# A Mamba-2 layer on one core: front end on 256 tokens, convolution without a halo, y channel-major to the output projection, exponent factors placed by DMA

## What is computed

```python
xn = _layernorm(x)
out = x + attn(xn) + tanh(xn @ W1.T @ W2.T @ W3 + bias)      # the three-matrix branch

# attn:
z, xBC, dt = split(xn @ W_in, [512, 512 + 768])              # 8 values of dt, one per head
dt = softplus(dt + dt_bias)
xBC = silu(causal_conv(xBC, conv_w, 4 taps) + conv_b)
x, B, C = split(xBC, [512, 512 + 128])                       # x: 8 heads of 64
a = -exp(A_log)
y = ssd(x * dt, dt * a, B, C) + x * D                        # decaying state of 128 x 64 per head
y = y * silu(z)
y = y * rsqrt(mean(y * y) + EPS) * rms_w
h = xn + y @ W_out
return _layernorm(h) * ln_g + ln_b
```

## Time and profile before

| | |
|---|---|
| median of 3 runs | 756.85 us (755.51 to 758.68) |
| span of the profiled execution | 754.5 us |
| PE busy | 732.5 us, 5412 products |
| PE weight loads busy | 626.0 us |
| DVE busy | 699.9 us, 1568 instructions |
| ACT busy | 671.5 us, 1715 instructions |
| POOL busy | 644.3 us, 1226 instructions |
| data moved | 20.13 MB, 27 GB/s |

### The profile page before, as it was taken

One profiled execution on the slowest core, in us unless ns is written; L12 is line 12 of the kernel. 1 busy time (PEld: TensorE's weight loads), 2 busy tenths in 40 slices (PEclk: granted clock), 3 DMA queues, 4 the chain that ended last, 5 costly groups with the idle time before them and its releaser, 6 DMA issues. The chain is left out here.

```text
span 754.5 us, 19295 instructions
## 1 busy us (share of the span) xinstructions
PE 732.5 (97%) x5412; PEld 626.0 (83%) x5412; DVE 699.9 (93%) x1568; ACT 671.5 (89%) x1715; POOL 644.3 (85%) x1226
## 2 busy tenths in 40 slices
PE   5899999999999999999999999999999999999994
PEld 5778888888888888888888888888888888888873
DVE  3779999999999999999999999999999999999996
ACT  4798899999999999999999999999999999999993
POOL 6666989889888989888988988888988888988865
PEclk8899999999999999999999999999999999999999
DMA  6000010000000000000000000000000000000001
GB/s 203 17 1 15 14 45 4 28 30 29 28 28 13 15 28 28 28 28 28 0 28 28 28 28 28 0 28 28 28 28 28 11 17 28 28 28 14 14 1 42
DMA packets 21417, 20.13 MB, mean 27 GB/s; under 512 B 2832, under 2 KB 20880, under 8 KB 21392
## 3 DMA queue, kind: packets, MB, share of 16 engines
q1 hardware_dynamic: 20176, 19.82, 8.1%
q10 hardware_dynamic: 1216, 0.02, 0.1%
HBM read 11.45 MB, written 8.39 MB: 26 GB/s over the span
## 5 line engine op out<-in xcount | busy, mean ns | idle before, releaser
L849 DVE SCALAR_TENSOR_TENSOR u<-ring,cw,u 128x256 f32<-128x256 f32 x561 | 252.5, 478 | 3.3 <-ACT u L1425 0.6
L1753 PE MATMUL ring<-xhl,wh 128*128 128x262 f32 x748 | 153.0, 296 | 0.5 <-ACT vabs L1417 0.4
L1753 PE MATMUL ring<-wh,xhl 128*128 128x512 f32 (+1 forms) x512 | 147.6, 348 | 0.5 <-ACT gate L1445 0.4
L1753 PEld LDWEIGHTS ring<-xhl,wh 128*128 128x128 f32 x748 | 122.3, 191 | 12.6 <-DVE u L849 7.5
L1425 ACT ACTIVATE u<-ring,cb,cw 128x256 f32<-128x256 f32 x187 | 107.5, 576 | 26.1 <-PE ring L1753 23.8
L1485 ACT ACTIVATE xdt<-xt_bank,dts 128x64 f32<-128x64 f32 x512 | 111.2, 336 | 0.0
L1753 PE MATMUL ring<-xhl,wl 128*128 128x262 f32 x374 | 106.7, 285 | 0.0
L1753 PEld LDWEIGHTS ring<-wh,xhl 128*128 128x128 f32 x512 | 90.6, 189 | 10.9 <-issue 1.2
L869 DVE SCALAR_TENSOR_TENSOR lay<-e_bank,btg 128x512 f32<-128x512 f32 x125 | 85.9, 687 | 12.5 <-ACT e_bank L1468 10.3
L1753 PE MATMUL ring<-wl,xhl 128*128 128x264 f32 (+1 forms) x256 | 87.2, 341 | 0.0
L1468 ACT ACTIVATE e_bank<-e_bank 128x512 f32<-128x512 f32 x125 | 75.5, 604 | 2.4 <-PE e_bank L1877 1.1
(11 more groups left out here) (203 smaller groups left out, 2111.7 us busy)
## 6 DMA issues: line engine op xcount, KB each, us to landing
xin<-in_x_dram SPq DMA_DIRECT2D x32, 256.0 KB, 2.9
out_dram<-obuf SPq DMA_DIRECT2D x31, 256.0 KB, 3.0
lay<-in_w_in_dram SPq DMA_DIRECT2D x1, 776.0 KB, 5.1
lay<-in_w_in_dram SPq DMA_DIRECT2D x1, 512.0 KB, 9.9
wo<-in_w_out_dram SPq DMA_DIRECT2D x1, 512.0 KB, 5.7
lay<-in_f2t_dram SPq DMA_DIRECT2D x1, 256.0 KB, 6.7
lay<-in_f_dram SPq DMA_DIRECT2D x1, 256.0 KB, 8.6
lay<-in_f1t_dram SPq DMA_DIRECT2D x1, 256.0 KB, 8.9
```

The costliest lines, as they stand in the source:

```text
L849: v.scalar_tensor_tensor(out=u[:, ct], in0=conv_bank(k, ct)[:, :, t:t + P], scalar=cw[:, ct, t:t + 1], in1=u[:, ct], op0=ALU.mult, op1=ALU ...
L1753: last = mul(out, a, c, start=first and i == 0, stop=i == n - 1)
```

## The change

- A step now is 256 tokens (`C = 2` chunks of 128) for the front end: 16 steps, two buffers, a loop body for two steps. Norm scale, `transpose_x`, convolution, z, softplus and `sums` work on 256 tokens at once; the back end still goes chunk by chunk.
- No halo: `conv_project` makes 512 columns (2 sequences x 256). `conv_in` writes to `xs[..., 0:T]` and `tap` adds the bank's 512 columns into `xs` at an offset, so that the last three columns spill over its end; `save_spill` (POOL) keeps them and `join_spill` (DVE) adds them to the next step's first three columns. `u` is gone.
- The gate is made channel-major (`z_project`: four groups of 128 channels). y stays channel-major: `y_off` is four products of 128 channels each; `scale_off` multiplies with `grow`, the growth factor laid out for each channel and token; POOL's `join_skip` adds `x * D` to it; `add_diag` adds that to y; `apply_gate` works in PSUM; `y_skip`, `y_tokens`, `transpose_y` are gone. There is one `yd_bank`, two `e_bank`.
- Squares: `y_split` (ACT) writes `yts` and the squares, `fold` (DVE) adds four channel tiles in two additions, `square_sum` (PE) sums over the partitions, `mean_square` (DVE) adds EPS.
- `sums` (ACT) writes rows and their Exp (`growth`). SP places the factors: `spread_factors`, 16 transfers of 2 KB from `rows` into `left` and `right`, for each chunk, in place of `spread_rows`; `put_growth` writes `growth` to DRAM, and `spread_growth` reads it back, repeated for 64 partitions, two transfers of 128 KB for each chunk and sequence.
- Output is stored from `res`; `obuf` is gone.

The core of the diff (the orders of all engines are written anew; only the pieces that the text speaks of are shown):

```diff
-PH = HALO + P
+C = 2
+T = C * P
-BUF = 3
+BUF = 2
...
-            def y_tokens(k, q):
-                pe.wait_ge(t2_done[q], k + 1)
-                for ki in range(KI):
-                    last = tr(yd_bank[q][:, ki * P:(ki + 1) * P], yct[:, q, ki * P:(ki + 1) * P], ident[:, :])
-            def transpose_y(k, q):
...
-                v.scalar_tensor_tensor(out=u[:, ct], in0=conv_bank(k, ct)[:, :, t:t + P], scalar=cw[:, ct, t:t + 1],
-                                       in1=u[:, ct], op0=ALU.mult, op1=ALU.add).then_inc(tap_done[ct], 1)
+                to = xs[:, b, ct, :, HALO - t:HALO - t + T]
+                v.scalar_tensor_tensor(out=to, in0=conv_bank(j, ct), scalar=cw[:, ct, t:t + 1], in1=to,
+                                       op0=ALU.mult, op1=ALU.add).then_inc(tap_done[ct], 1)
...
+            def scale_off(j, b, c, q):
+                k = C * j + c
+                dve.wait_ge(yoff_in_psum[q], k)
+                dve.wait_ge(grow_loaded[q], 32 * k)
+                dve.wait_ge(y_done[q], k)
+                v.tensor_tensor(t1[:, q], xt_bank[:, :], grow[:, q].rearrange("p k t -> p (k t)"), ALU.mult).then_inc(t1_done[q], 1)
+            def fold(j, b, c, q):
+                v.tensor_tensor(sq[:, q, 0:2], sq[:, q, 0:2], sq[:, q, 2:4], ALU.add).then_inc(folded_done[q], 1)
+                dve.wait_ge(folded_done[q], 2 * k + 1)
+                v.tensor_tensor(folded[:, q], sq[:, q, 0], sq[:, q, 1], ALU.add).then_inc(folded_done[q], 1)
...
+                for ct in range(KI):
+                    block_of = slice(ct * P, (ct + 1) * P)
+                    last = mul(xt_bank[:, block_of], state[:, q, block_of], xs[:, b, KI + 1, q, tokens(c)], start=True, stop=True)
...
+                mul(ss_bank[:, q], folded[:, q], ones[:, 0:2], start=True, stop=True).then_inc(ss_in_psum, 1)
...
+            def exponents(j, b, c, q, half):
+                pe.wait_ge(factors_in[c], 256 * (j + 1))
...
+            def spread_factors(j, b, c):
+                k = C * j + c
+                sp.wait_ge(rows_done, j + 1)
...
+                for i in range(FOUR):
+                    for low in range(2):
+                        at, n = c * Q * H, 2 * FOUR * i + FOUR * low
+                        sp.dma_start(right[n:n + FOUR, c, i].bitcast(F32), rows[at + i:at + Q * H:FOUR, b, low].bitcast(F32)).then_inc(factors_in[c], 16)
+                        sp.dma_start(left[LO + n:LO + n + FOUR, c, i].bitcast(F32),
+                                     rows[at + FOUR * i:at + FOUR * (i + 1), b, low].bitcast(F32))\
+                            .then_inc(factors_in[c], 16)
+            def spread_growth(j, b, c, q):
...
+                for i in range(2):
+                    sp.dma_start(grow[i * HD:(i + 1) * HD, q], of_half[i].partition_broadcast(HD)).then_inc(grow_loaded[q], 16)
```

The new order on SP for one step, then PE from `sums` to the end of its `one_pass`, then the start of PE's `one_pass`:

```diff
+            def one_pass(j, b, b1):
+                spread_growth(j - 1, b1, 0, 0)
+                spread_growth(j - 1, b1, 0, 1)
+                spread_factors(j - 1, b1, 1)
+                spread_growth(j - 1, b1, 1, 0)
+                store(j - 2, b, 0)
+                spread_growth(j - 1, b1, 1, 1)
+                store(j - 2, b, 1)
+                load_again(j + 2, b, 0)
+                load_again(j + 2, b, 1)
+                put_growth(j, b)
+                spread_factors(j, b, 0)
...
+                sums(j, b)
+                z_project(j, b, 0)
+                y_off(j - 1, b1, 1, 1)
+                conv_project(j, b, 5)
+                out_project(j - 1, b1, 0, 1)
+                x_tokens(j, b, 0, 0)
+                z_project(j, b, 1)
+                y_diag(j - 1, b1, 1, 1)
...
+                states(j - 2, b, 1, 1)
+                z_project(j - 1, b1, 2)
+                b_and_g(j - 1, b1, 0, 0)
+                z_project(j - 1, b1, 3)
+                b_and_g(j - 1, b1, 0, 1)
+                y_off(j - 1, b1, 0, 0)
+                square_sum(j - 2, b, 1, 0)
+                square_sum(j - 2, b, 1, 1)
+                exponents(j - 1, b1, 0, 0, 1)
```

More of the change, by code:

```diff
@@ L52 @@
 GROUPS = Q * H // GH
+FOUR = 4
 LO = 32
[L54 to L55 removed]
 LOG_TERMS = 5
@@ L355, in _ @@
+            passes(sp, head, one_pass, tail)
+            for b in range(BUF):
+                for c in range(C):
+                    sp.wait_ge(stored[b * C + c], 16 * (steps // BUF) + 16 * (b * C + c == BUF * C - 1))
         @block.gpsimd
@@ new lines, in head @@
+                square_sum(0, 0, 0, 0)
+                square_sum(0, 0, 0, 1)
+                exponents(0, 0, 1, 0, 0)
+                x_tokens(0, 0, 1, 1)
+                exponents(0, 0, 1, 1, 1)
+                out_project(0, 0, 0, 0)
+                exponents(0, 0, 1, 1, 0)
+                states(0, 0, 1, 0)
+                sums(1, 1)
+                conv_project(1, 1, 5)
+                y_off(0, 0, 1, 1)
+                y_diag(0, 0, 1, 0)
+                out_project(0, 0, 0, 1)
@@ new lines, in head @@
+                x_tokens(2, 0, 0, 0)
+                z_project(2, 0, 1)
+                z_project(2, 0, 2)
+                y_diag(1, 1, 1, 1)
+                b_and_g(2, 0, 0, 0)
+                states(1, 1, 1, 1)
+                b_and_g(2, 0, 0, 1)
+                z_project(2, 0, 3)
+                y_off(2, 0, 0, 0)
+                square_sum(1, 1, 1, 0)
+                square_sum(1, 1, 1, 1)
+                exponents(2, 0, 0, 0, 0)
+                out_project(1, 1, 1, 0)
+                exponents(2, 0, 0, 0, 1)
@@ new lines, in head @@
+                exponents(2, 0, 1, 1, 1)
+                square_sum(2, 0, 0, 1)
+                y_diag(2, 0, 1, 0)
+                x_tokens(2, 0, 1, 1)
+                conv_project(3, 1, 4)
+                conv_project(3, 1, 0)
+                out_project(2, 0, 0, 0)
+                states(2, 0, 1, 0)
+                sums(3, 1)
+                z_project(3, 1, 0)
+                y_off(2, 0, 1, 1)
+                conv_project(3, 1, 5)
+                out_project(2, 0, 0, 1)
+                x_tokens(3, 1, 0, 0)
```

3980 lines of the change are left out of this document (2519 added, 1461 removed).

## The result

The changed kernel takes 798.94 us (median of 4 runs, 795.32 to 799.91) against 756.18 us (754.74 to 758.68) for the kernel before: a ratio of 1.056 (95% interval 1.0528 to 1.0591). The forecast was 724.2 us in a range of 706 to 752. It was wrong in sign and by 75 us. The profiled execution has a span of 797.4 us.

The account below looks back on a forecast made before the run. PE was taken as the bound at 22.40 us per chunk, DVE 1.6 us behind. The new period, between 20.6 and 21.7, was taken as 21.1: 32 x 21.1 + 46.6 = 721.8, with 2.35 more 724.2 us, range 706 to 752.

Parts of the forecast that it names:

- filling and draining: Start and end of the kernel: first back end waits longer, two chunks end uncovered; +9 taken, so 46.6 us.
- part (3): DVE: fold additions of about 0.48 and 0.2 us, for two sequences +1.4 us per chunk.
- the late queue: SP: slow factor issues make the growth 3.2 us late in each of 16 steps, 775 us; chance 0.15.
- the second rival: DVE becomes the bound with all of its waits, 21.7 us per chunk, 743 us in all; chance 0.18.
- PE, 41.2 us per step: TensorE's work: from 22.40 to 20.6 us per chunk of 128 tokens, a step being two chunks.
- convolution and z: PE: 512-column convolution groups -0.3, z groups with swapped operands +0.1, together -0.2 us per chunk.
- unchanged: PE: exponents, states, `y_diag`, `out_project` and branch keep their cost; fewer switches before `out_project` -0.05 us per chunk.
- DVE's work: DVE: taps, `y_skip`, folds and small operations together take its work from 20.8 to 20.1 us per chunk.
- factor issues 0.6 or more apart: SP: sign that would show the forecast wrong, with PE waiting for transfers; expected distance 0.5 us.

Follow-up runs that it names:

- e10: The changed kernel with one reduction for the fold, loop written out and eight 4 KB factor transfers per chunk for sixteen: 742.41 us, ratio 0.9825.
- e4: The changed kernel with one reduction in place of the fold's two additions and the loop written out: 754.89 us, ratio 0.9971.
- e15: The fastest version (742.4 us) with the fold's two additions back in place of the reduction: 771.0 us, ratio 1.0205.
- e3: The changed kernel with its loop over two steps written out, both fold additions kept: 775.08 us, ratio 1.0239.
- e1: The changed kernel with one reduction in place of the fold's two additions, loop kept: 768.92 us, ratio 1.0161.
- e13: The fastest version (742.4 us) with the loop put back, four rounds of four chunks: 758.09 us, ratio 1.0032.
- e14: The fastest version (742.4 us) with two rounds in the loop and the others written out: 748.72 us, ratio 0.9885.
- e16: The kernel before with six chunks in the loop body instead of three, four rounds, last three chunks written out: 774.27 us, ratio 1.0234.

## Why the prediction was wrong, point by point

**The sum that closes.** With the prices of the causes put back alone into e10: 742.4 + 28.6 (additions) + 15.7 (loop) + 12.5 (sixteen issues, e4 against e10) = 799.2, against 798.9 measured. Taken out of the changed kernel instead, they were 30.0, 23.9 and 2.0. That is 55.9, against 56.5 us in all. So the three account for the distance from 742.4 to 798.9. That the sum closes within 0.3 us is luck, since the executions of e15 alone are 8 us apart. And a single price depends on what else is there: the additions cost 20.2 us between e3 and e4, the loop 14.0 between e1 and e4, the sixteen issues 2.0 or 12.5. From there to the forecast of 724.2 are 18.2 us: 16 steps at 43.5 instead of 42.2 are 21, and 43.9 us of filling and draining (739.9 - 16 x 43.5) instead of 46.6 are -2.7.

**DVE, part (3), the folds: the step that failed worst.** The 0.48 and 0.2 us were right for a fold that stands alone (starts 0.45 and 0.21 apart). But they were taken without asking what runs on GpSimd meanwhile. What it takes lay in the rows, though none of them shows such a meeting, since the kernel before has additions with both inputs in SBUF on DVE only at its start and end: an addition of GpSimd on 512 elements is 1.29 us, POOL is busy for 89 of 100 us, and the fold is, but for the 12 columns of `join_spill`, the only work of DVE in the changed kernel's steady part with both inputs in SBUF; taps, `weigh`, `scale_off`, `y_low` and the rest have one in PSUM. And the fold stands on TensorE's path with no cover, since `square_sum` comes next and `out_project` behind it. The Trainium skill states the rule, in SBUF — State Buffer, Who interferes with whom: a VectorE instruction with two SBUF inputs and a GpSimd instruction that reads SBUF shut each other out for a whole instruction; one with at most one SBUF input, outside the two-port modes, doesn't. The trace agrees: 1.05 and 1.24 us against 0.41 and 0.29, and 1.07 for the reduction. As a rival it would have read: one meeting per step, some 1.5 us, 16 times, 24 us; the runs gave 20.2 to 30.0, by what else was in the kernel.

The same happens to `join_spill`, priced at 0.2 us per chunk and measured at 0.6 (20.0 us of busy time for the 48 of the changed kernel). Its 12 columns with both inputs in SBUF take 0.15 us alone, but once in most steps of the changed kernel 0.8, because they end 0.03 us behind GpSimd's operation of L614 (1.04 us from 503.02).

```profile
503.29 0.80 DVE L1145 TENSOR_TENSOR xs<-xs,spill 128x12 f32<-128x12 f32 x1
```

It is there in e10 too (13.4 us in all), so it is no part of the sum above; what it costs the kernel was not tried.

**The loop: no step of the prediction at all.** The change made the body four chunks long where it was three, and the prediction took the body's length as free. It cost 14.0 to 23.9 us. The earlier trace rows could not show it, since the kernel before pays nothing for its jumps.

**SP, the late queue: mechanism right, place wrong.** The issue distance was forecast at 0.50 and is 0.62, beyond the 0.60 from which the rival was to decide. The growth came 16.0 us after the end of `sums`, where the rival had 16.8 and the forecast 13.4: the sixteen took 10.3 us where the rival had 10.9 and the forecast 8.0. Yet the rival's 51 us were wrong: it multiplied 3.2 us of lateness by 16 steps as if DVE reached `scale_off` on time. In the changed kernel DVE is late itself and the queue costs 2 us; with the rest cleared, 12.5. The rows had a steady distance only for large transfers (0.37 to 0.38 of length), and the value taken, 0.50 from the start of the kernel, was too low by a quarter. The Trainium skill's 0.68 us for a transfer of 4 KB (DMA: Bandwidth & Descriptors, Bandwidth), which the prediction had set beside it, was nearer: the 4 KB transfers of e10 are 0.68 to 0.77 apart (three of 225 more). The page gives it for the length of a transfer from HBM that GpSimd issues, not for the distance of SP's issues, so this may be chance. (The prediction calls that outcome the second rival's; its 10.9 us belong to the third, the late queue.)

**PE, 41.2 us per step: mis-sized by 2.3.** Measured from start to start over one step of e10 (507.54 to 551.07, 43.53) against two periods of the kernel before (44.83, first start to last):

| per 256 tokens, us | before | e10 | change | forecast |
|---|---|---|---|---|
| convolution and z | 15.05 | 15.10 | +0.05 | -0.4 |
| `transpose_y`, `y_tokens` | 3.01 | 0 | -3.01 | -3.0 |
| `sums` | 1.34 | 0.87 | -0.47 | -0.66 |
| `square_sum` | 0 | 0.78 | +0.78 | +0.6 |
| `y_off` | 3.56 | 3.40 | -0.16 | 0 |
| `y_diag` | 3.79 | 4.09 | +0.30 | 0 |
| exponents, with the hole before `sums` | 3.21 | 3.55 | +0.34 | 0 |
| `x_tokens` | 1.41 | 1.81 | +0.40 | 0 |
| branch | 3.10 | 3.44 | +0.34 | 0 |
| the rest | 10.36 | 10.49 | +0.13 | -0.1 |
| sum | 44.83 | 43.53 | -1.30 | -3.6 |

The removed transposes are as priced, as both figures come from the kernel before. The largest single miss of this table is convolution and z: the 512-column groups gained nothing, where 0.4 had been forecast. `sums` and `square_sum` were 0.2 short each. The other half is the word "unchanged": `y_diag` was one group of 32 products and is two of 16; `x_tokens` and the exponents now stand next to groups that wait 0.1 to 0.4 us for a bank, as `sums` does and `out_project` below, which starts when `last_h` of the other sequence has ended (525.09); the branch group takes the rest of `states` in front of it (1.82 in place of 1.55). With the right 43.5 the sum would have read 16 x 43.5 + 46.6 + 2.4 = 745, 3 us from e10. Two of these rows of e10, `x_tokens` with four transposes (0.65 to the next start, where the earlier trace rows has 0.35 for four) and `y_diag` with 16 products:

```profile
524.59 0.60 PE L2711 MATMUL xt_bank<-ident,xs 128*128 128x128 f32 x4
525.24 0.36 PE L2625 MATMUL bg_bank<-woh,yts 128*128 128x256 f32 x1
...
526.83 1.09 PE L2785 MATMUL yd_bank<-lay,xdt 128*64 128x128 f32 x16
```

**DVE's work, POOL, filling: right; ACT nearly.** DVE is busy for 96.4% of 43.5 us in e10, 41.9, of which 1.6 are what four reductions take over four pairs of additions: 40.3 against a forecast of 40.2. Taps are 0.66 apart (forecast 0.65), `conv_in` takes 0.79 us (0.78 to 0.84), 16 and 15 table loads (one of each kind per step), `y_off` 0.81 to 0.89 for four blocks, POOL 37.3 us per step of e10 (85.8% of 43.5; forecast 37), ACT 35.8 (82.2%; forecast 34), filling and draining 43.9 us (46.6).

**The signs to look for.** Of what was to prove it wrong, "factor issues 0.6 or more apart" came true and was not the main cause; that PE would wait for a fold, or that every second step would be longer, stood on neither list.

## What to carry to other kernels

Before adding a VectorE operation with both inputs in SBUF, look at what GpSimd runs beside it and who waits for the result; here operations with one input from PSUM (0.67 to 0.70 us on 512 elements, whatever GpSimd did) and a reduction over one input (0.96 to 1.09) kept their length, though the reduction's own is greater. When a change makes a hand-written loop body longer, time it with the loop written out before blaming the work in it. And when several causes stand behind one another, undoing one in the slow kernel underprices the one that is hidden (2.0 against 12.5 us): put each back alone into the fastest version, and see whether the sum closes.

## What the runs showed of the hardware that was not expected

- An addition of VectorE with both inputs in SBUF that comes while a GpSimd operation with two inputs in SBUF is under way ends a fixed time behind it: 0.28 us for 256 elements, 0.15 for 128, 0.03 for 12. The 128 elements, 0.29 us alone, so take 1.24 to 1.29 beside an operation of 1.27 to 1.32.
- A jump back is free with a body of three chunks (8 jumps, 0.0003 of the time), where the trace has no instruction transfers, and costs 4 to 8 us each with bodies of four or six (e13 15.7 for three, e14 6.3 for one, e16 17.8 for three, the changed kernel 23.9 for three); VectorE stands with "issue", 8.2 us in three times in e16.
- After a hole on PE the granted clock can stay at 1.2 GHz (0.50) for some us. In the changed kernel PE had waited 1.14 us for the fold at 660.34; the clock of the stretches from 662 on:

```profile
662.00:663.00 1.00, 1.00 (x7) 1.00 (x7) 0.20 (x1) 0.00 (x0) 1.00 (x2) 0.53 0.02 4
663.00:664.00 1.00, 1.00 (x6) 0.82 (x6) 0.57 (x2) 0.24 (x1) 1.00 (x3) 0.50 0.01 4
...
666.00:667.00 1.00, 1.00 (x16) 0.87 (x17) 0.45 (x1) 0.36 (x2) 0.47 (x2) 1.00 0.01 2
```

The products of `out_project` start 0.21 us apart there and 0.12 at full clock. From `square_sum` to `y_diag` it is 6.04 us here (660.34 to 666.38), and 4.79 at full clock behind the same hole of 1.14 us one step earlier (615.17 to 619.96): the clock cost 1.25 us, and it does not fall behind every such hole. So a hole can cost more than its length. The pairs of e15, 8 us apart at mean clocks of 0.981 and 0.970, fit that; no run separates the two parts.

- Small transfers are issued by SP 0.62 us apart at 2 KB and 0.68 to 0.77 at 4 KB, against 0.37 to 0.38 us of length for the 256 KB loads: halving their number helps, making them smaller hardly does.
- `square_sum` as four FP32 products with two columns in place of one costs 1.4 us per step (777.86 - 754.89 over 16 steps), and the same four in FP32R 1.6 less (777.86 - 752.49).
